# Selective-scan and mixture-of-experts kernel on one Trainium2 core: the last five blocks' results combined in idle tiles, the last post stage on its own table, the rank mask ahead of the gate weights

## The reference

```python
xz = einsum('bld,ed->ble', layernorm(x), in_proj_w); x_ssm, z = split(xz, 2)
x_conv = silu(causal depthwise convolution of x_ssm with 4 taps + conv_b)
Bm, Cm, delta = split(x_conv @ x_proj_w.T)        # 16, 16, 1 columns
delta = softplus(delta); A = -exp(A_log)          # A: 512 x 16
h = exp(dt * A) * h + dt * Bt * xt; y = sum_n h * Ct      # for each token in order
x = x + einsum((y + D_param * x_conv) * silu(z), out_proj_w)
t = layernorm(x)
probs = softmax(t @ router_w.T + router_b); top_p, top_i = top_k(probs, 2)
w = top_p / (sum(top_p) + EPS)
out = sum over the 2 choices of w * (t @ expert_weights[top_i])   # 8 experts, 512 x 512
x = x + out / clip(sum(w), EPS) * (1 + sum(w) * EPS)
```

## Time and profile before

| | us |
|---|---|
| median of 3 runs | 2971.43 |
| lowest and highest | 2971.4, 2974.65 |
| the profiled execution | 2975.89 |
| its span (first to last instruction) | 2974.1 |
| TensorE busy | 2415.0 (81%) |
| VectorE busy | 2278.7 (77%) |
| GpSimd busy | 1811.8 (61%) |
| ScalarE busy | 1486.8 (50%) |
| mean granted TensorE clock | 0.875 |

### The profile page before, as it was taken

The page is one execution under the profiler, slowest core; times in us unless marked ns, Lnnn a source line. Parts: engine busy times, 40 slices in busy tenths (PEclk is TensorE's granted clock), DMA queues, the critical chain, the costliest instruction groups (busy, mean ns, idle before and its releaser), DMA issues.

```text
span 2974.1 us, 34543 instructions
## 1 busy us (share of the span) xinstructions
PE 2415.0 (81%) x9510; PEld 1401.4 (47%) x9510; DVE 2278.7 (77%) x3189; ACT 1486.8 (50%) x2417; POOL 1811.8 (61%) x1420
## 2 busy tenths in 40 slices
PE   5668686798979898898979898898979898887754
PEld 2335353455545554555545554545545554444421
DVE  3889888898888888888888898888888888665100
ACT  3454545465555556455655546465645556342210
POOL 2455766566566767576676767577675767574412
PEclk8778777798989999898989898899979898899977
DMA  3762411223233434334343434344343434455735
GB/s 123 243 244 92 142 54 57 85 86 117 72 113 105 144 103 125 116 108 141 108 122 106 139 111 133 105 119 130 115 126 98 150 103 131 124 161 157 192 97 129
DMA packets 192570, 366.27 MB, mean 123 GB/s; under 512 B 22912, under 2 KB 22912, under 8 KB 192384
## 3 DMA queue, kind: packets, MB, share of 16 engines
q1 hardware_dynamic: 144272, 263.26, 27.4%
q0 software_dynamic: 28672, 67.13, 10.6%
q10 hardware_dynamic: 19440, 33.69, 3.1%
HBM read 212.73 MB, written 151.26 MB: 122 GB/s over the span
## 4 chain that ended last, share of the span: by engine, by line
PE 47%; DVE 19%; issue 13%; ACT 7%; DMA 7%; POOL 6%; SPq 0%; DVEq 0%; POOLq 0%; ACTq 0%
PE work L1094 34%; DVE h L919 8%; PE hT L1099 7%; DVE acc L927 6%; PE work L1099 3%; POOL u L646 3%; DMA x_out<-result_scratch,rows_of 3%; PE work L1154 2%; ACT decay L783 2%; DVE xc L950 1%; DMA b_ring<-b_scratch 1%; DMA xe<-row_scratch 1%; ACT L783 1%; POOL x_out L750 1%; DMA result_scratch<-ye 1%
## 5 line engine op out<-in xcount | busy, mean ns | idle before, releaser
L646 POOL TENSOR_TENSOR u<-xc,b_ring 128x1024 f32<-128x1024 f32 x512 | 1229.8, 2411 | 757.2 <-DVE h L919 576.0
L783 ACT ACTIVATE decay<-dt,neg_a 128x512 f32<-128x512 f32 x1024 | 700.8, 689 | 690.1 <-DVE h L919 675.0
L1099 PE MATMUL hT<-ident,h 128*128 128x128 f32 x4096 | 693.4, 305 | 364.6 <-DVE acc L927 290.4
L1099 PEld LDWEIGHTS hT<-ident,h 128*128 128x128 f32 x4096 | 524.7, 156 | 650.3 <-DVE acc L927 285.5
L1094 PE MATMUL work<-w_exp,xeT 128*128 x1528 | 749.1, 636 | 37.4 <-DVE dt L962 13.6
L927 DVE SCALAR_TENSOR_TENSOR acc<-hT,ct,acc 128x512 f32<-128x512 f32 x960 | 699.8, 729 | 86.9 <-PE hT L1099 83.9
L919 DVE TENSOR_TENSOR_SCAN h<-decay,h_last,u 128x512 f32<-128x512 f32 x512 | 652.7, 1275 | 114.1 <-ACT decay L783 77.8
L919 DVE TENSOR_TENSOR_SCAN h<-decay,u 128x512 f32<-128x512 f32 x512 | 621.4, 1215 | 123.6 <-ACT decay L783 93.2
L1094 PE MATMUL work<-xnT,w_in 128*128 128x512 f32 x1024 | 484.2, 618 | 2.2 <-DVE dt L962 1.5
L1094 PEld LDWEIGHTS work<-w_exp,xeT 128*128 128x128 f32 x1528 | 295.5, 204 | 366.8 <-issue 366.1
L750 POOL DMA_INDIRECT x_out<-result_scratch,rows_of x120 | 192.7, 1606 | 184.9 <-DMA x_out<-x_scratch 91.0
(11 more groups left out here) (145 smaller groups left out, 1856.7 us busy)
## 6 DMA issues: line engine op xcount, KB each, us to landing
b_ring<-b_scratch SPq DMA_DIRECT2D x256, 256.0 KB
xe<-row_scratch SPq DMA_DIRECT2D x165, 256.0 KB
result_scratch<-ye SPq DMA_DIRECT2D x165, 256.0 KB
row_scratch<-x_out ACTq DMA_DIRECT2D x32, 1024.0 KB, 4.8
x<-in_x SPq DMA_DIRECT2D x66, 256.0 KB, 5.4
x_scratch<-x SPq DMA_DIRECT2D x64, 256.0 KB, 2.0
xn<-in_x SPq DMA_DIRECT2D x62, 256.0 KB, 3.4
x_out<-x_scratch SPq DMA_DIRECT2D x60, 256.0 KB, 3.1
```

Source lines behind the costliest of these rows:

```text
L646: nc.gpsimd.tensor_tensor(out=u[:, at:at + 2, :], in0=xc[:, half, 2 * k:2 * k + 2, :], in1=b_ring[:, n % ROWS:n % ROWS + 1, :].to_broadcas ...
L783: nc.scalar.activation(decay_bank[g % 2][:], dt[:, half, :], ACT.Exp, scale=neg_a[:, c, n:n + 1]).then_inc(decay_ready, 1)
L1099: last = nc.tensor.transpose(ps[:, k * P:(k + 1) * P], tile(k), ident[:])
```

## The change

1. *Combining.* Blocks 0 to 10 are combined as before, in iterations 5 to 15. The last five (11 to 15, `LATE`) no longer go through `x_out`: their x1 tiles are fetched into tiles that have come free, four row tiles at once (block 11 into `xnT` in iteration 15, blocks 12 and 13 into the two halves of `h` in 16, block 14 into `u` in 17, block 15 into `x1`), all four gathers of the first choice are issued and then all four of the second, and each row tile has a semaphore of its own (`late_row`). In iteration 17 the fetches and gathers of block 14 stand ahead of the third tile's load, and the stores behind the eighth tile.
2. *Result buffers.* `result_scratch` has three parts in place of two, and `rows_store` waits for the group three back to be combined.
3. *Last post stage.* Iteration 16 takes its post steps from a table of its own, `POST_END`. Its weighed first-choice rows go to `xc` in place of the single `x_first`, so that a weighing waits for no earlier scatter.
4. *Group tables.* `new_group` for block 14 stands at the end of iteration 15 (place 66.9) and no longer at place 6 of iteration 16.
5. *Rank mask.* The five mask instructions stand first in `gate_weights`, and wait only for `gate_top`.
6. *Places.* All numbers in `COMBINE`, `POST`, `PREP` and the three expert tables are new; for most steps they move by less than three places.

```diff
-    COMBINE_PLAN = {j: [j - 5] for j in range(5, BLOCKS - 1)}
-    COMBINE_PLAN[BLOCKS - 1] = [BLOCKS - 6, BLOCKS - 5]
-    COMBINE_PLAN[BLOCKS] = [BLOCKS - 4, BLOCKS - 3]
-    COMBINE_PLAN[BLOCKS + 1] = [BLOCKS - 2]
-    COMBINE_PLAN[BLOCKS + 2] = [BLOCKS - 1]
-    NEW_GROUP = {first + n + 1: g for g, (first, n) in enumerate(GROUPS)}
+    COMBINE_PLAN = {j: j - 5 for j in range(5, BLOCKS)}
+    LATE = 5
+    NEW_GROUP = {first + n + 1: g for g, (first, n) in enumerate(GROUPS[:-2])}
...
-        "gather": [18.41, 23.94, 30.99, 34.63, 50.48, 53.97, 61.4, 66.9],
-        "store": [25.16, 38.24, 56, 64.91],
+        "gather": [19.21, 20.41, 33.06, 35.43, 48.33, 52.85, 53.39, 61.42],
+        "store": [26.24, 36.34, 57.92, 64.13],
-        "gate_top": [28.77],
-        "gate_exp": [31.68],
-        "gate_weights": [37.97],
-        "rank": [40.13],
-        "scatter": [45.9, 48.02, 55.57, 61.9],
+        "gate_top": [32.08],
+        "gate_exp": [34.84],
+        "gate_weights": [37.11],
+        "rank": [39.92],
+        "scatter": [46.48, 50.71, 55.56, 66.9],
-        "b_store": [45.82],
+        "b_store": [53.72],
...
-        "end_rows_load": [4.4, 4.87, 9.38, 14.21, 19.3, 22.88, 23.71, 28.64, 30.95, 32.51, 38.05, 41.7, 46.29, 46.9, 46.96],
+        "end_rows_load": [0, 0, 10.08, 14.05, 21.27, 21.64, 23, 25.59, 31.55, 32.99, 34.08, 35.8, 43.23, 48.29, 49.92],
+        "end_gate_exp": [33.91],
+        "end_gate_weights": [63.88],
+        "end_rank": [45.07],
+        "end_weigh": [39.87, 51.21, 58.42, 63.4],
+        "end_scatter": [65.9, 66.5, 66.5, 66.9],
+        "middle_new_group": [66.9],
+        "far_fetch": [30.07, 33.2, 34.66, 35.31],
+        "far_gather": [43.54, 44.99, 49.4, 52.4, 59.1, 59.44, 60.5, 65.5],
+        "mid_gather": [20.55, 21.08, 21.38, 21.38, 21.57, 23.46, 25.01, 25.09],
+        "near_gather": [52.1, 52.34, 52.49, 52.71, 53.89, 56.66, 58.75, 58.85],
+            steps += late_in("far", 0) + [(COMBINE_LATE["middle_new_group"][0], ("new_group", len(GROUPS) - 2))]
...
+    def late_in(kind, of):
+        places = COMBINE_LATE[kind + "_fetch"], COMBINE_LATE[kind + "_gather"], COMBINE_LATE[kind + "_store"]
+        return ([(at, ("late_fetch", of, q)) for q, at in enumerate(places[0])] +
+                [(at, ("late_gather", of) + index) for index, at in zip(INDEX["late"], places[1])] +
+                [(at, ("late_store", of, q)) for q, at in enumerate(places[2])])
+
     def combine_in(j):
-        blocks = len(COMBINE_PLAN.get(j, []))
-        return [((at + i * N * C) / blocks, (kind, i * Q + s[0]) + tuple(s[1:])) for i in range(blocks) for at, (kind, *s) in steps_in(COMBINE)]
+        steps = [(at, (kind, s[0]) + tuple(s[1:])) for at, (kind, *s) in steps_in(COMBINE)] if j in COMBINE_PLAN else []
+        if j == BLOCKS - 1:
+            steps += late_in("far", 0) + [(COMBINE_LATE["middle_new_group"][0], ("new_group", len(GROUPS) - 2))]
+        if j == BLOCKS:
+            steps += late_in("mid", 1) + late_in("near", 2)
+        return steps
+
+    def post_in(j):
+        if j == BLOCKS:
+            return [(at, (kind.split("_", 1)[1], i)) for kind, places in POST_END.items() for i, at in enumerate(places)]
+        return steps_in(POST) if 1 <= j < BLOCKS else []
...
     def closing_steps(j):
+        def late(kind, of):
+            if kind == "late_gather":
+                return [(kind, of) + index for index in INDEX["late"]]
+            return [(kind, of, q) for q in range(Q)]
         if j == BLOCKS + 2:
-            return ([("gather", q, 0) for q in range(Q)] + [("gather", q, 1) for q in range(Q)] + [("store", q) for q in range(Q)])
+            return late("late_gather", 4) + late("late_store", 4)
         count = EXPERT_PLAN[j][2]
-        tiles = [[("rows_load", 0), ("rows_load", 1), ("rows_T", 0), ("rows_load", 2), ("rows_evict", 0)]]
+        steps = [("new_group", len(GROUPS) - 1), ("rows_load", 0), ("rows_load", 1)] + late("late_fetch", 4) + late("late_fetch", 3) + late("late_gather", 3)
+        steps += [("rows_T", 0), ("rows_load", 2), ("rows_evict", 0)]
         for i in range(count):
-            tiles += [[("rows_T", i + 1)] * (i + 1 < count) + [("rows_load", i + 3)] * (i + 3 < count) +
-                      [("rows_evict", i + 1)] * (i + 1 < count) + [("expert", i), ("expert_evict", i), ("rows_store", i)]]
-        rows = [[("fetch", q), ("gather", q, 0), ("gather", q, 1), ("store", q)] for q in range(Q)] + [[("fetch_last", q) for q in range(Q)]]
-        steps = [("new_group", 0)]
-        for i, tile in enumerate(tiles):
-            steps += tile
-            steps += rows[i // 3] if i % 3 == 0 and i // 3 < len(rows) else []
+            steps += [("rows_T", i + 1)] * (i + 1 < count) + [("rows_load", i + 3)] * (i + 3 < count)
+            steps += [("rows_evict", i + 1)] * (i + 1 < count) + [("expert", i), ("expert_evict", i), ("rows_store", i)]
+            steps += late("late_store", 3) if i == count // 2 else []
         return steps
...
-        res_dram = [nc.dram_tensor(f"result_scratch{i}", [RESULTS, D], fp32, kind="Internal").ap() for i in range(2)]
+        res_dram = [nc.dram_tensor(f"result_scratch{i}", [RESULTS, D], fp32, kind="Internal").ap() for i in range(3)]
...
+        def late_tile(of, q):
+            return (xnT[:, q, :], h[:, 0, q, :], h[:, 1, q, :], u[:, q, :], x1[:, q, :])[of]
+
+        def x_first_of(r, q):
+            return xc[:, 0, q, :] if r == BLOCKS - 1 else x_first[:]
+
+        def wait_combined(eng, g):
+            if g < 0:
+                return
+            first, n = GROUPS[g]
+            early = min(first + n, BLOCKS - LATE)
+            for k in range(2):
+                eng.wait_ge(gathered[k], 16 * TOP * Q // 2 * early)
+            for i in range((first + n - early) * Q):
+                eng.wait_ge(late_row[(max(first, early) - BLOCKS + LATE) * Q + i], 16 * TOP)
...
+                    elif s[0] == "late_fetch":
+                        of, q = s[1], s[2]
+                        block = BLOCKS - LATE + of
+                        if of == 0:
+                            wait_product(sync, BLOCKS - 2, ("z_project", C - 1, 1))
+                        elif of < 3:
+                            sync.wait_ge(hT_ready, (BLOCKS * N + of - 2) * Q)
+                        elif of == 3:
+                            sync.wait_ge(scanned, BLOCKS * N * C)
                         else:
-                            sync.wait_ge(last_gathered[q], 16 * TOP)
-                            sync.dma_start(out[first:first + P, :], x1[:, q, :]).then_inc(stored[q % 2], 16)
+                            sync.wait_ge(scattered[q], 16 * BLOCKS)
+                        sync.wait_ge(x1_stored[q], 16 * (block + 1))
+                        first = block * T + q * P
+                        sync.dma_start(late_tile(of, q), x1_dram[first:first + P, :]).then_inc(late_loaded[of], 16)
...
+                        wait(pool, rows_ready, r)
+                        pool.wait_ge(gate_step, (r + 1) * GATE_STEPS)
+                        link(nc.gpsimd.tensor_tensor(out=mask[:], in0=pick[:, tiles, 0, :], in1=pick[:, tiles, 1, :], op=ALU.add))
+                        link(nc.gpsimd.tensor_tensor(out=before[:, 1, :], in0=before[:, 0, :], in1=mask[:, 0, :], op=ALU.add))
+                        link(nc.gpsimd.tensor_tensor(out=before[:, 2, :], in0=before[:, 1, :], in1=mask[:, 1, :], op=ALU.add))
+                        link(nc.gpsimd.tensor_tensor(out=before[:, 3, :], in0=before[:, 2, :], in1=mask[:, 2, :], op=ALU.add))
+                        link(nc.gpsimd.tensor_tensor(out=after, in0=before[:, 3, :], in1=mask[:, 3, :], op=ALU.add))
+                        pool.sem_inc(mask_ready, 1)
...
+                    elif s[0] == "late_gather":
+                        of, q, k = s[1], s[2], s[3]
+                        g, pos = GROUP_OF[BLOCKS - LATE + of]
+                        if q == 0 and k == 0:
+                            pool.wait_ge(table_step, (g + 1) * TABLE_STEPS)
+                            done_tiles(pool, rows_stored, FIRST_TILE[g + 1])
+                        if k == 0:
+                            pool.wait_ge(late_loaded[of], 16 * Q)
                         else:
-                            pool.wait_ge(loaded, 16 * (BLOCKS + 1))
-                        nc.gpsimd.indirect_dma_start(row, None, res_dram[g % 2][:, :],
+                            pool.wait_ge(late_row[of * Q + q], 16)
+                        nc.gpsimd.indirect_dma_start(late_tile(of, q), None, res_dram[g % 3][:, :],
                                                      bass.IndirectOffsetOnAxis(ap=rows_of[g % 3][:, pos * Q + q, k:k + 1], axis=0),
-                                                     compute_op=ALU.add).then_inc(ready, 16)
+                                                     compute_op=ALU.add).then_inc(late_row[of * Q + q], 16)
...
+                        if r < BLOCKS - 1:
+                            wait(act, first_scattered, 16 * (r * Q + q))
```

(4 more changed lines are left out.)

204 lines of the change are left out of this document (110 added, 94 removed).

## The result

The changed kernel took **2899.24 us** (median of 4, 2896.86 to 2902.32), the kernel before beside it 2971.41 us: ratio 0.9743, 95% interval 0.9717 to 0.9768. That is 72.2 us less, where 2902 and -69 were forecast, inside the range of 2872 to 2932. The profiled execution took 2902.32 us, its span 2900.3 (before 2975.89 and 2974.1).

The account below looks back on a forecast made before the run. Behind the last scan stand 272 us, only 165 of them TensorE's, with loads held behind stores in SyncE's queue. Terms -48 - 8 - 9 - 4 = -69 us from 2971.4 gave 2902 us, range 2872 to 2932.

Parts of the forecast that it names:

- Iteration 17: First load to last expert product: block 14's four turns leave SyncE's queue, 116.4 to 68 us; -48 (-52 to -34).
- The stall taken as 4 us: Iteration 17: loads delayed by sharing DMA engines with eight gathers, between no stall and 18.5 us; 4 us taken.
- Gap to iteration 17: Last product of iteration 16 to first load of 17: earlier gathers, weighing into `xc`; -8 us (-11 to 0).
- Start of iteration 16: Group table moved to iteration 15's end, so the output projection starts sooner; -9 us (-13 to -3).
- other branch: Start of iteration 16: the table between `y_skip` steps delays y_gate, for which the projection waits; gates done at 2719.
- Rest of iteration 16: The 88.0 us from projection to last product lose a 2.8 us load wait and a cold stretch; -4 (-9 to +5).
- Repeating iterations: Full iterations with new places: same instructions, only neighbours change; 0 us, with ends of -15 and +30.
- second rival: New places gain 1 us in each repeating iteration, from (a): 2887 us; chance 0.11.
- (a): Repeating iterations: last gather and store earlier, so SyncE no longer stands before the next `b_ring` loads; at most 1 us each.
- (b): Repeating iterations: gate exponent and weights 10 us closer, against 8.2 us of slack; GpSimd stall 0 to 2 us.
- first rival: Repeating iterations: GpSimd's gate and `u` come late, 1 to 2 us in each of 15; about 2924 us; chance 0.15.
- fourth rival: Repeating iterations: GpSimd waits at the sum until its `u` lead is gone; slower, 6 us each gives 2992; chance 0.03.

Follow-up runs that it names:

- the two exchanges: COMBINE, POST, PREP and EXPERTS places swapped up to iteration 14: old ones in the changed kernel, 2910.43 us; new ones in the kernel before, 2973.24 us.
- the run with the old table: Changed kernel with only the old COMBINE places (fetches, gathers, stores of results) in iterations up to 14: 2895.02 us, ratio 0.971.

## Why the prediction was right

The terms' errors are -5.1, -0.9, +5.0, -3.4, -0.8 and +0.3, together -4.9 in the span. That the total came out within 3 us of the forecast is luck in part: two terms missed by 5 us in opposite directions.

*Iteration 17* (-48, measured -48.8). The four turns were the whole loss: taken out alone -48.6, put back alone +49.9. The stall taken as 4 us came out at 3.3, by the 67.6 us against 64.3 without one: the first product took 5.91 us instead of 5.25, the transposes of tile 2 waited 0.47, and the rest are single tiles of 4.0 to 4.6 us where 3.87 was counted. Fetches and gathers in a line, window by window (columns as in the earlier trace rows; the last row is the closing gathers):

```profile
2808.70:2819.00 10.30, 8.21 (x19) 4.06 (x20) 0.00 (x0) 1.79 (x3) 0.31 (x1) 0.61 0.84 301
2819.00:2834.50 15.50, 14.97 (x45) 6.98 (x44) 0.00 (x0) 3.96 (x7) 12.15 (x8) 1.00 0.95 209
2878.20:2895.00 16.80, 0.00 (x0) 0.00 (x0) 0.00 (x0) 0.00 (x0) 12.39 (x8) 0.50 0.81 128
```

Eight gathers beside a load and a store per tile fill the DMA engines to 0.95, and TensorE is busy 14.97 of 15.5 us all the same: two tiles of lead were enough, as the estimate had it. The third load was issued at 2813.16 and its transposes could start at 2818.67, 5.5 us later, where the first took 2.8; TensorE waited 0.47 us of it. The prediction took the fetches' time less the cover as about nothing, and that was right. By the Trainium skill (DMA: Bandwidth & Descriptors, "Two DMAs through the same engine are not ordered"), descriptors of one queue of one DMA engine start in order, so a later landing behind the fetches is what one would see. The trace agrees with its 5.5 us against 2.8, but loads that only share the DMA engines with the fetches could look the same; no run tells the two apart.

*Gap to iteration 17* (-8, measured -11.4). Right in kind: old places alone bring back 7.6 of it. But the prediction did not say which of the things in the old gap held the load. It was not the last scatter, issued at 2818.95, but once more the store of a combined tile. The chain that ended last in the kernel before, and its counterpart after:

```profile
2826.24 4.80 DMA x_out<-result_scratch,rows_of
2831.06 0.34 SPq L584
```

```profile
2803.53 2.72 DMA row_scratch<-x,row_at
```

So the old gap had the same cause as iteration 17's turns, and only after the change does the last scatter set it, as the sum assumed. By the sum the load comes 10 us behind product 13; it came 8.4 behind it (2798.71 to 2807.13), since the scatter landed in 2.72 us and not in 4.64. Behind product 14 it is 3.4 instead of 6.5, as that product ended 5.0 us behind product 13 where 3.5 were counted. The gap of the old order is itself no fixed number: in the two kernels that keep iteration 16 of before it is 13.0 (iteration 17 done alone) and 11.8 us (new places in the kernel before), so 2 to 3 of the 11.4 are spread. The weighing into `xc`, named as one of the two reasons, was none in the profiled execution: with `x_first` the gap is the same 3.4 us.

*Start of iteration 16* (-9, measured -9.9). The table's place alone, undone, costs 11.8. The end of the forecast's path was right: the first expert tile's load and product, then the projection. Its other branch, over `y_skip` and the gates, was not the one that counted: with the table back in its old place the gates are done 7.7 us ahead of the projection, and in `after` at 2713.19, 1.6 us ahead of it. The forecast had the product cold, that is at the lower of TensorE's two granted clocks; it ran in 3.70 us, where it took 5.49 before.

*Rest of iteration 16* (-4, measured +1.0): the mis-sized term, inside its bounds. The cold stretch that was to go is there, in other products. TensorE:

```profile
2740.63 5.39 PE L1180 MATMUL work<-w_exp,xeT 128*128 x8 [1.43 <-ACT xeT L976]
...
2755.71 5.19 PE L1180 MATMUL work<-w_exp,xeT 128*128 x8 [0.90 <-DVE logit L1082]
```

Two products at 5.2 to 5.4 instead of 3.7 us are 3.2 us. The wait of 2.8 us for a load became one of 1.4.

*Repeating iterations* (0, measured -5.1 in the profile, a gain of 5 to 12 us by the two exchanges). The second rival was partly true in size; the forecast's bounds of -15 to +30 held it, and the spread between executions, some 5 to 10 us with the same code, is as large. The reasons given were not the ones. The gain in the profile is made before block 6, and 3.6 us of it in iteration 0, not by about 1 us in each of 15. (a) SyncE's places at the iteration's end are worth nothing, as the run with the old table shows. (b) The gate did move as said:

```profile
2271.24 0.17 DVE L1101 TENSOR_REDUCE prob_sum<-prob 128x4 f32<-128x32 f32 x1
...
2272.47 0.27 POOL L776 TENSOR_TENSOR mask<-pick 128x32 f32<-128x32 f32 x1
```

GpSimd starts 1.2 us behind the sum instead of 8.2, and does not wait for it: the slack shrank to what was forecast, and stopped there. The sign of the first rival is in the waits, from 700 to 2500:

```profile
DVE h L1007 <- POOL u L722: 49.3, 26, 3.0
```

In the same stretch of the kernel before it is 14.4 us in 9 waits. VectorE waits 35 us more for `u`, yet it is as busy as before in these 1800 us (1540.1 us, before 1539.2). Other waits of its own went: those for `hT` (`acc` behind TensorE) fell from 51.9 to 33.6 us, and those for the output projection (`x`, the residual) from 40.3 us in 11 waits to none. So the first and fourth rival named a wait that did grow but cost no time; GpSimd, by whose wait for `prob_sum` it was to come, has no such wait in the stretch.

## What to carry to other kernels

When a queue issues in order, look for waits whose cost is not their own but that of what stands behind them: here the store of a finished tile held up the loads of unfinished ones. Moving the stores behind the loads, which takes a buffer and a semaphore for every tile in flight, made the tail 49 us shorter with the same transfers; with the buffers but in the old order nothing was gained. In a tail without a scan such waits are the path; in the steady part the same queue waited 48 us more without a loss, so find out first which stretch has no lead. And before an instruction is moved forward on an in-order engine, list what it passes: one early `row_of` that waits for another engine put a stop of 9.1 us on TensorE, in a kernel that was meant to be 5 to 9 us shorter.
